# Latent attention on one core: query twins copied by DMA inside SBUF, low halves of the queries subtracted on GpSimd

## The reference, cut to what matters

```python
q_blhd = jnp.einsum('bld,dhk->blhk', x_bld, Wq)               # 16 heads of 64
latent_bll = jnp.einsum('bld,dc->blc', x_bld, Wkv_down)       # 64 latent features
k_blhd = jnp.einsum('blc,chk->blhk', latent_bll, Wk_up)
v_blhd = jnp.einsum('blc,chk->blhk', latent_bll, Wv_up)
attn = jnp.einsum('bqhd,bkhd->bhqk', q_blhd, k_blhd) / jnp.sqrt(64)
attn = jax.nn.softmax(jnp.where(mask, attn, neg_inf), axis=-1)   # causal mask
y_blhd = jnp.einsum('bhqk,bkhd->bqhd', attn, v_blhd)
return jnp.einsum('bqhd,hdo->bqo', y_blhd, Wout)
```

## Time and profile before

| | |
|---|---|
| median of 3 runs | 2813.07 us (2809.03 to 2814.67) |
| profiled execution, whole | 2811.18 us |
| its span, first to last instruction | 2809.2 us |
| busy in the span: PE, DVE, ACT, POOL | 88%, 76%, 55%, 31% |
| latent attention, first key scores to end | about 1776 to 2612 us of the span |
| period of one batch (16 steps) in the loop | 102 to 106 us |

### The profile page before, as it was taken

The page is one execution under the profiler, slowest core; times in us unless marked ns, Lnnn a source line. Parts: engine busy times, 40 slices in busy tenths (PEclk is TensorE's granted clock), DMA queues, the critical chain, the costliest instruction groups (busy, mean ns, idle before and its releaser), DMA issues. The chain is left out here.

```text
span 2809.2 us, 39573 instructions
## 1 busy us (share of the span) xinstructions
PE 2459.3 (88%) x14385; PEld 1348.3 (48%) x14385; DVE 2127.2 (76%) x3928; ACT 1537.0 (55%) x2281; POOL 879.3 (31%) x859
## 2 busy tenths in 40 slices
PE   7999999989999998989999678588988888898467
PEld 3444444444444444434444357255654655565356
DVE  4489688888979887788924466589788879787766
ACT  6655454555555464555555532277667667667422
POOL 4444344434433443444444610102112112112110
PEclk9999999999999999999999877799999999999778
DMA  5100000000000000000000100000000000000101
GB/s 179 60 1 1 0 1 1 1 1 1 1 1 1 1 1 1 1 1 1 1 1 1 50 16 1 1 2 2 2 2 3 2 2 2 2 2 2 50 16 61
DMA packets 29167, 33.09 MB, mean 12 GB/s; under 512 B 6404, under 2 KB 25396, under 8 KB 28964
## 3 DMA queue, kind: packets, MB, share of 16 engines
q1 hardware_dynamic: 27988, 27.88, 3.1%
q0 software_dynamic: 976, 2.56, 0.3%
HBM read 25.58 MB, written 4.19 MB: 11 GB/s over the span
## 5 line engine op out<-in xcount | busy, mean ns | idle before, releaser
L757 POOL TENSOR_TENSOR g_lo<-g_full,g_hi 128x512 f16<-128x512 f32 x512 | 668.2, 1309 | 903.7 <-ACT g_hi L849 902.2
L849 ACT ACTIVATE g_full<-hid,b_col 128x512 f32<-128x512 f32 x512 | 351.6, 687 | 562.9 <-PE hid L152 561.4
L150 PE MATMUL hid<-y_hi,w_hi 128*128 128x512 f16 x1024 | 397.1, 388 | 38.9 <-DVE y_lo L835 34.9
L151 PE MATMUL hid<-y_lo,w_hi 128*128 128x512 f16 x1024 | 396.2, 387 | 0.0
L152 PE MATMUL hid<-y_hi,w_lo 128*128 128x512 f16 x1024 | 395.9, 387 | 0.0
L150 PE MATMUL acc<-g_hi,w_hi 128*128 128x512 f16 x1024 | 389.9, 381 | 5.2 <-POOL g_lo L757 5.2
L151 PE MATMUL acc<-g_lo,w_hi 128*128 128x512 f16 x1024 | 389.6, 380 | 0.0
L152 PE MATMUL acc<-g_hi,w_lo 128*128 128x512 f16 x1024 | 389.4, 380 | 0.0
L849 ACT ACTIVATE g_hi<-hid,b_col 128x512 f16<-128x512 f32 x512 | 348.8, 681 | 0.0
L2226 DVE TENSOR_REDUCE mla_m_col<-mla_ps 128x1 f32<-128x512 f32 (+3 forms) x512 | 224.8, 482 | 60.5 <-PE mla_ps L2068 52.2
L2364 ACT ACTIVATE mla_p_full<-mla_ps 128x1280 f32<-128x1280 f32 x128 | 158.4, 1237 | 142.7 <-PE mla_ps L2098 142.3
(11 more groups left out here) (376 smaller groups left out, 4844.6 us busy)
## 6 DMA issues: line engine op xcount, KB each, us to landing
latent_stage<-in_L_ffn_w_dram SPq DMA_DIRECT2D x16, 512.0 KB, 4.7
x<-in_L_attn_x_dram SPq DMA_DIRECT2D x8, 512.0 KB, 8.4
routed_w<-in_L_ffn_w_dram SPq DMA_DIRECT2D x4, 1024.0 KB, 8.0
out_dram<-x SPq DMA_DIRECT2D x8, 512.0 KB, 3.6
mla_sums<-mla_sum_row SPq DMA_DIRECT2D x128, 2.0 KB
latent_stage<-in_L_attn_Wq_dram SPq DMA_DIRECT2D x1, 1024.0 KB, 6.5
latent_stage<-in_L_attn_Wout_dram SPq DMA_DIRECT2D x1, 1024.0 KB, 8.9
routed_wqkv<-in_L_ffn_wq_dram SPq DMA_DIRECT2D x2, 256.0 KB, 2.9
```

The source lines that it names most:

```text
L150: pe.matmul(out, w_hi, v_hi, start=first, stop=False)
L151: pe.matmul(out, w_hi, v_lo, start=False, stop=False)
L757: pool.tensor_tensor(g_lo[:, g, :], g_full[:, g, :], g_hi[:, g, :], ALU.subtract).then_inc(tail_done, 1)
L849: act.activation(out[:, g, :], hid[:, ht % 4, :], ACT.Gelu, bias=b1_col[:, ht:ht + 1], scale=1.0 / WS).then_inc(gelu_done, 1)
```

## The change

- ACT writes the high half of head h+8 into partitions 0 to 63 and that of head h+9 into partitions 64 to 127, each in the partitions that its query has in PSUM. It then writes a third time: a float32 copy of the whole pair, `q_full` (128x512, two buffers), and counts it in `q_copied`. Before that copy it waits for the low halves of the pair two pairs back, which read the same buffer.
- SP issues the twins as DMAs from the half of `q_hi` that ACT wrote to the other half, 64 partitions of 1 KB each, behind the DMA of the sums in its step. Four semaphores count them.
- POOL subtracts `q_hi` from `q_full` for the low halves, two instructions of 64x512 at the end of its step.
- DVE no longer does the copies and subtractions.
- PE's waits for bank 6 are now for `q_copied` (ACT) in place of `q_tail`; the wait before the key-row scores stays on `q_tail`, which POOL now counts; the wait for a twin is now for its DMA.

```diff
@@ tiles and semaphores
+        q_full = sb("q_full", [P, 2, SEQ])
-        q_twin = sem("q_twin")
+        q_twin = [[sem(f"q_twin{i}{j}") for j in range(2)] for i in range(2)]
+        q_copied = sem("q_copied")
@@ queries_read (PE)
-                pe.wait_ge(q_tail, n)
+                pe.wait_ge(q_copied, n)
...
-                pe.wait_ge(q_tail, min(n, BATCH * H))
+                pe.wait_ge(q_copied, min(n, BATCH * H))
@@ tensor_step, queries of a pair
-                    pe.wait_ge(q_tail, hn)
+                    pe.wait_ge(q_copied, hn)
@@ tensor_step, query-row scores
-                pe.wait_ge(q_twin, hn + 1)
+                pe.wait_ge(q_twin[hh % 2][hh // 2 % 2], 16 * (hb * (H // 4) + hh // 4 + 1))
@@ vector_step
-            hb, hh, hn = head_of(b, h + LEAD)
-            if exists(hb) and h % 2 == 0:
-                for i in range(2):
-                    ring = (hh + i) % RING
-                    own = slice(i * LATENT, (i + 1) * LATENT)
-                    dve.wait_ge(q_head, hn + i + 1)
-                    dve.tensor_copy(q_hi[LATENT:P, ring, :], q_hi[0:LATENT, ring, :]).then_inc(q_twin, 1)
-                    if i == 1:
-                        dve.wait_ge(q_twin, hn + i + 1)
-                    dve.scalar_tensor_tensor(q_lo[0:LATENT, ring, :], ps[own, 6, :], 1.0 / WS, q_hi[own, ring, :],
-                                             ALU.mult, ALU.subtract).then_inc(q_tail, 1)
@@ scalar_step
                 for i in range(2):
-                    act.activation(q_hi[0:LATENT, (hh + i) % RING, :], ps[i * LATENT:(i + 1) * LATENT, 6, :], ACT.Copy,
+                    own = slice(i * LATENT, (i + 1) * LATENT)
+                    act.activation(q_hi[own, (hh + i) % RING, :], ps[own, 6, :], ACT.Copy,
                                    scale=1.0 / WS).then_inc(q_head, 1)
+                if not isinstance(hn, int) or hn >= 4:
+                    act.wait_ge(q_tail, hn - 2)
+                act.activation(q_full[:, hh // 2 % 2, :], ps[:, 6, :], ACT.Copy, scale=1.0 / WS).then_inc(q_copied, 2)
@@ pool_step, at its end
+            hb, hh, hn = head_of(b, h + LEAD)
+            if exists(hb) and h % 2 == 0:
+                pool.wait_ge(q_copied, hn + 2)
+                for i in range(2):
+                    ring, own = (hh + i) % RING, slice(i * LATENT, (i + 1) * LATENT)
+                    if i == 1:
+                        pool.wait_ge(q_tail, hn + 1)
+                        if exists(before) and SPREAD_AT <= h < SPREAD_AT + MLA_PAIRS:
+                            pool.wait_ge(o_tail, MLA_PAIRS * before + h - SPREAD_AT + 1)
+                    pool.tensor_tensor(q_lo[0:LATENT, ring, :], q_full[own, hh // 2 % 2, :], q_hi[own, ring, :],
+                                       ALU.subtract).then_inc(q_tail, 1)
+                pool.wait_ge(q_tail, hn + 2)
@@ dma_step, behind the DMA of the sums
+            hb, hh, hn = head_of(b, h + LEAD)
+            if exists(hb) and h % 2 == 0:
+                for i in range(2):
+                    ring = (hh + i) % RING
+                    own, twin = (slice(j * LATENT, (j + 1) * LATENT) for j in (i, 1 - i))
+                    sp.wait_ge(q_head, hn + i + 1)
+                    sp.dma_start(q_hi[twin, ring, :], q_hi[own, ring, :]).then_inc(q_twin[i][hh // 2 % 2], 16)
```

## The result

The changed kernel takes 2763.6 us (median of 4 runs, 2762.2 to 2764.9), against 2811.2 us for the kernel before in the same comparison (4 runs, 2809.0 to 2814.7). The ratio is 0.983, with a 95% interval of 0.981 to 0.985: 47.6 us off, or 46.9 between the two profiled spans (2809.2 and 2762.3 us). The forecast was 2770, 43 off, so the total is close. Stage by stage it is less close.

A forecast was written before the change was run, and what follows sets the result against it. The layer runs at PE's pace plus what DVE adds. Gains of 26 (loop), 2 (batch 7), 3 (batch 0), 5 (batch -1) and 7 (clock) sum to 43 us off, for a median of 2770; range 2741 to 2808.

The forecast's parts named there:

- One batch: Loop batch: shorter PE waits, summed step by step, gain 4.9 us, less 0.5 for ties: 4.4 net.
- ties of the value product: Odd steps: value product can start about 4.0 us after the scores, PE there at 4.1 to 4.2; 0.5 us per batch off.
- the cover of POOL's subtractions: POOL's two subtractions take 2.4 us, `p_lo` starts 2.4 us after the same moment: near miss, a hit costs 0.1 to 0.3.
- Steps 5 and 7: Step 5: chain of exponentials, `y_hi`, `y_lo`, fourth maximum stays; of 2.28 us only some 0.8 comes back. Step 7 likewise chained.
- Maxima at 40 us: PE's waits for the maxima over the layer fall from 70.5 to about 40 us, mostly 0.52 each.
- Prologue: Batch -1, where PE has nothing to fill waits: 1.5 us from each of three pairs, about 5 us gained.
- Last batch: Batch 7 has queries in its first half alone: 2 us gained, apart from the clock.
- Clock in the loop: Clock drops behind the 1.73 us wait, in four batches, go with that wait: 4 x 1.7 = 7 us.
- Twins: Twin DMAs land in 2.2 us against 3.1 available in the tightest case, so one step's work hides them.
- Rival 1: POOL's second subtraction delays `p_lo` 0.6 to 1.2 us in 40 odd steps: 36 us given back, 2806 us; chance 0.24.
- Rival 2: All PE waits for DVE go except the 0.52 us ones: 75 us off with clock, time 2738; chance 0.09.
- Rival 3: Twins land 5 us after their high half, PE stands 1.9 us in 40 odd steps: 2846 us; chance 0.10.

The follow-up runs named there:

- e5_turn: Changed kernel, with ACT writing `y_hi` between its two exponentials in steps 5 and 7 instead of behind both: 2753.7 us.
- e11_pause_b3: Kernel before, plus a barrier and three unused DVE reductions between the latent attention and the routed layer behind: 2814.4 us, ratio 1.000.
- e7_late: Changed kernel, with each twin's DMA also waiting until POOL has subtracted that head's low half: 2807.2 us.
- e3_ballast: Changed kernel, with three unused DVE reductions of 128x512 per pair where the copies and subtractions were: 2782.6 us.
- e6_both: Changed kernel, with `y_hi` between the exponentials in steps 5 and 7, and POOL's step 0 subtractions held until DVE's inverse is done: 2745.0 us.

## Why the prediction came out as it did

- **Which waits go.** Right. Those for `q_lo` are gone; steps 15 and 3 are as worked out, the wait of 1.30 in step 9 went; DVE, ACT and the batch (96.0 to 96.4 us) are in the places given.
- **One batch.** 4.4 us net was forecast, and undisturbed batches fell from 101.3 to 96.0: 5.2. The starts of the key-row scores in one such batch (from 2323.55 us before, 2288.20 after) split 5.0 of it:

| steps | predicted | measured |
|---|---|---|
| 15 to 2 | 1.7 | 1.0 |
| 3 | 0.8 | 0.8 |
| 4 and 5 | 0.2 | 0.4 |
| 6 to 8 | 0.7 | 0.8 |
| 9 and 10 | 1.5 | 2.0 |
| 11 to 14 | 0 | 0 |
| ties of the value product | -0.5 | 0 |

  Errors of both signs cancel. The wait of step 1 was to be 0.52 and is 1.09 to 1.56. The step that failed is the one on the cover of POOL's subtractions. I had asked only whether they meet `p_lo`, found a near miss, and not gone through what else DVE does while POOL reads. They do graze `p_lo`, by 0.3 to 0.4 us in step 3 (the mean of all 128 hides it: 1593 ns, 1602 before, because `o_lo` holds `p_lo` a little less than before), and they lengthen the inverse in step 1 by 1.5 to 1.8 us. The 0.5 taken off for ties in the value product was too much: PE waits 0.3 us for `p_lo` in the whole layer.
- **Steps 5 and 7.** The chain is shown by `e5_turn`. Step 5 was to keep about 1.5 of 2.28 us and keeps 0.56 + 1.28 = 1.84.
- **Maxima at 40 us.** Wrong: 57.9. It assumed that nearly every remaining wait is 0.52; those of steps 1, 5 and 7 are two to three times that in each batch. For step 5 this follows from the prediction's own chain, and the figure of 40 had forgotten it.
- **Prologue.** Mis-sized: 5 was forecast, 10.1 measured. PE's waits there fell by 3.6 us, from 15.7 to 12.0, less than forecast; the other 6.5 go with matmuls at the lower clock (starts 0.43 us apart in place of 0.22), which I had not counted. Windows of the same stretch, before and after:

```profile
1790.00:1800.00 10.00, 5.78 (x22) 2.54 (x22) 5.60 (x13) 1.22 (x3) 0.00 (x0) 0.66 0.00 0
```

```profile
1790.00:1800.00 10.00, 6.98 (x51) 3.79 (x50) 5.65 (x14) 3.55 (x6) 2.29 (x2) 1.00 0.06 14
```

  The granted clock went from 0.66 to 1.00. The waits that remain there are short, and some are for a twin, as the prediction's 1.5 us per pair allowed:

```profile
1786.81 0.28 PE L2069 MATMUL mla_ps<-mla_key_hl,mla_q_hi 128*128 128x256 f16 x1 [0.79 <-DVE mla_m_col L2228]
...
1787.98 0.39 PE L2069 MATMUL mla_ps<-mla_key_hl,mla_q_hi 128*128 128x512 f16 x1 [0.83 <-DMA mla_q_hi<-mla_q_hi]
```

- **Last batch.** 2 and one drop of the clock (2) forecast, 6.9 measured. In windows of 10 us from its border the clock before was 0.83, 1.00, 0.83, 0.97 and 0.86, so there was more than one drop; in the changed kernel it is 1.00 in the first seven. But the trace before is one execution: `e11_pause_b3` has the same instructions up to the end of the layer, its other batches are within 0.5 us of before's, and its last batch took 81.9 us and not 85.5, with one window of 0.83. Against that the gain is 3.3 us, near the forecast. So about half of the 6.9 is a matter of the single execution.
- **Clock in the loop.** The drops behind the wait in step 1 went, though the wait did not: none stands behind the waits of up to 1.56 us. Before, the same wait of 1.73 us had a drop behind it in three of the six loop batches and none in the other three, so the wait alone doesn't decide it, and that the drops went as forecast is partly luck. The loop gave 34.5, against 26 + 5 = 31 (three of the four drops named in the prediction lie in it, the fourth in the last batch). Two batches of after keep 101 us. At the end of them PE stands for 3 us, and the window of 2080 to 2090 us has a clock of 0.83; the kernel before has such waits as well (3.01 and 2.91 us). The profile names no cause, but the place is telling: the loop on the engines covers two batches in a pass, so it goes back to its start twice, and these are the first matmuls of its second and third pass, in every kernel here (2.9 to 3.6 us), with DVE held by 1.5 us or more beside them. The prediction left them out, rightly, as nothing in the change touches them:

```profile
2084.50 0.39 PE L2096 MATMUL mla_ps<-mla_q_hi,mla_key_hl 128*128 128x512 f16 x1 [3.14 <-issue]
```

- **Twins.** Right. 64 KB land in 1.9 us, 2.7 at most (2.2 taken), issue takes 0.53 (0.63 taken), and in the loop no step waits; the slack of 3.1 is shown by `e7_late`. The estimate from the Trainium skill, DMA: Bandwidth & Descriptors, Anatomy of one DMA, whose figures are for DMAs issued by GpSimd, was 2.15 us; the 1.9 measured for SyncE is somewhat less.
- **Rival 1** has the right mechanism and the wrong size: `p_lo` is held for 0.3 to 0.4 us once in a batch, not for 0.6 to 1.2 in every odd step, and two other instructions are held for 1.5 to 1.8 us together. **Rival 2** is false: the chains of steps 5 and 7 stayed. **Rival 3** is false: in the loop a twin is issued some 0.3 us after its high half and lands 1.9 us later, 2.2 in all, and the point from which that rival decides was 4.2.
- **The layer behind.** Not in the working at all. 9.0 us were lost there; without them the time would have been some 2755.

The total is close by luck: 12 us too little in the layer stand against 9 us lost behind it that I did not look for.

## What to carry to other kernels

When work goes to GpSimd, list every instruction of VectorE that runs while it reads SBUF, small ones too, and not only the long one; an instruction of 0.2 us becomes one of 1.2. But before repairing such a hit by a delay, look at what runs where the work then lands: here the repair moved the hit from two small instructions to `p_lo` and won nothing, while moving one ACT instruction ahead of an exponential (`e5_turn`) won 10 us. Ask of each step taken off a busy engine what waits for its place in the queue, not only for its time; and where an idle stretch of PE is shortened in a part with little other work, read the granted clock there and put it into the sum.

## What the runs showed of the hardware

- POOL's subtraction of 64x512 takes 1.15 us, as that of 128x512 does alone: half the partitions save nothing. ACT's float32 copy of 128x512 out of PSUM takes 0.60 us, as its copies of 64x512 do.
- A VectorE instruction of 128x64 that meets a GpSimd subtraction ends with it: 1.02 and 1.22 us in place of 0.20 and 0.22, and back again when GpSimd starts later. A copy of 64x512 goes from 0.29 to 1.20 us, the subtraction of 128x1280 from 1.48 to 2.41. A reduction of 128x512 (`e3_ballast`) stays at 669 to 689 ns.
- The same instructions of one layer took 161.6 to 170.6 us, with the granted clock in the same window at 1.00 or 0.50. A difference of 8 us in this kernel's median can therefore come from a stretch that the edit does not touch (`e5_turn` and `e6_both`: layers of 812.4 and 812.0 us, medians 8.7 apart), and from one execution to the next (`e6_both`: 2744.9 and 2752.7).
